# Gated attention and expert layer on one core: two full-width products written as four products of 32 weights' columns

## The reference, cut to what matters

```
x: (128, 64, 128)   ctx: (128, 64, 128)   16 heads of 8, all fp32
xn  = layernorm(x)
qh, kh, vh = heads(xn @ W_q + b_q), heads(ctx @ W_k + b_k), heads(ctx @ W_v + b_v)
ctx_out = softmax(qh kh^T / sqrt(8)) vh               # within each of the 128 sequences of 64
x   = x + tanh(g_xattn) * (ctx_out @ W_o + b_o)       # "attention's output product"
f   = layernorm(x)                                     # 8192 rows
idx, score = argmax and max of softmax((f @ w_red) @ wg_n^T)      # one of 8 experts for each row
h   = gelu(f @ W1[idx] + b1[idx])                      # 128 -> 256, "first layer"
o   = (h @ W2[idx] + b2[idx]) * score                  # 256 -> 128, "second layer"
out = x + tanh(g_ffn) * o
```

## Time and profile before

| what | us |
|---|---|
| median of 3 runs | 360.19 |
| lowest, highest | 358.85, 363.16 |
| the profiled execution, whole | 359.64 |
| its span, first to last instruction | 357.2 |
| mean granted TensorE clock over the span | 0.974 |

### The profile page before, as it was taken

One profiled execution on the slowest core, in us unless ns is written; L12 is line 12 of the kernel. 1 busy time (PEld: TensorE's weight loads), 2 busy tenths in 40 slices (PEclk: granted clock), 3 DMA queues, 4 the chain that ended last, 5 costly groups with the idle time before them and its releaser, 6 DMA issues.

```text
span 357.2 us, 15462 instructions
## 1 busy us (share of the span) xinstructions
PE 311.2 (87%) x5630; PEld 234.2 (66%) x5630; DVE 285.5 (80%) x1024; ACT 240.9 (67%) x604; POOL 260.7 (73%) x417
## 2 busy tenths in 40 slices
PE   3978899998999899999999977677798999999950
PEld 1625766775775676776776655566687889998840
DVE  7787989889899989989999899978577666666620
ACT  3666699898889879999988973746333555555520
POOL 6585755386386888898899878786777777777771
PEclk9989999999999999999999999989989999999995
DMA  5344535334413423323212121251124443433110
GB/s 118 97 142 115 136 119 143 101 99 105 122 62 94 152 76 110 102 72 117 76 59 67 54 86 44 71 158 50 57 77 136 141 129 104 114 106 98 58 41 0
DMA packets 47157, 34.01 MB, mean 95 GB/s; under 512 B 9800, under 2 KB 42955, under 8 KB 47083
## 3 DMA queue, kind: packets, MB, share of 16 engines
q1 hardware_dynamic: 42440, 23.90, 24.1%
q0 software_dynamic: 4352, 9.00, 7.5%
q10 hardware_dynamic: 292, 0.13, 0.1%
HBM read 17.13 MB, written 10.04 MB: 76 GB/s over the span
## 4 chain that ended last, share of the span: by engine, by line
PE 57%; POOL 11%; DVE 10%; issue 9%; ACT 7%; SPq 2%; DMA 1%; POOLq 0%; DVEq 0%; ACTq 0%
PE m L1354 9%; PE sc L1326 8%; POOL records L437 6%; PE sc L1188 6%; PE pv L1263 6%; PE pv L1275 4%; PE m L1418 4%; PE m L1411 4%; PE sc L1198 3%; PE sc L1181 3%; DVE mx L1046 2%; PE m L1287 2%; POOL out L512 2%; PE m L1351 2%; ACT PT L636 2%
## 5 line engine op out<-in xcount | busy, mean ns | idle before, releaser
L1046 DVE TENSOR_REDUCE mx<-sc 128x8 f32<-128x512 f32 x128 | 82.1, 683 | 14.1 <-PE sc L1198 13.8
L512 POOL DMA_INDIRECT out<-fo,rr x71 | 69.8, 983 | 22.7 <-issue 20.6
L437 POOL DMA_INDIRECT records<-XR,pos x64 | 63.3, 990 | 17.0 <-issue 15.8
L636 ACT ACTIVATE PT<-sc 128x512 f32<-128x512 f32 x64 | 38.1, 595 | 21.2 <-issue 15.5
L1354 PE MATMUL m<-w,fgT 128*128 x280 | 49.7, 301 | 0.1
L1326 PE MATMUL sc<-fxT,w1s 128*128 128x128 f32 x276 | 44.2, 283 | 5.0 <-ACT fxT L619 2.6
L1025 DVE SCALAR_TENSOR_TENSOR fo<-m,rr 128x128 f32<-128x128 f32 x70 | 24.4, 349 | 27.1 <-PE m L1354 26.9
L1263 PE MATMUL pv<-PT,V 128*32 128x64 f32 x2048 | 42.6, 223 | 2.4 <-DVE NV L1066 1.4
L1326 PEld LDWEIGHTS sc<-fxT,w1s 128*128 128x128 f32 x276 | 37.1, 195 | 7.5 <-issue 4.4
L1188 PE MATMUL sc<-Qd,kT 32*128 32x128 f32 x1024 | 40.1, 273 | 0.0
L619 ACT ACTIVATE fxT<-sc 128x128 f32<-128x128 f32 x69 | 19.1, 277 | 31.1 <-PE sc L1314 30.5
(11 more groups left out here) (225 smaller groups left out, 729.4 us busy)
## 6 DMA issues: line engine op xcount, KB each, us to landing
rr<-records SPq DMA_DIRECT2D x71, 72.0 KB, 2.1
XC<-in_x SPq DMA_DIRECT2D x16, 256.0 KB, 4.3
C<-in_ctx SPq DMA_DIRECT2D x16, 256.0 KB, 3.7
Qd<-Qf SPq DMA_DIRECT2D x64, 64.0 KB, 1.9
Kd<-kb SPq DMA_DIRECT2D x64, 32.0 KB
w<-in_L_ffn_W SPq DMA_DIRECT2D x16, 128.0 KB, 2.8
out<-fo,rr POOLq DMA_INDIRECT x71, 2.3
w1l<-in_L_ffn_W SPq DMA_DIRECT2D x8, 128.0 KB, 3.7
```

What stands on the lines that cost most here:

```text
L437: nc.gpsimd.indirect_dma_start(out=records, out_offset=bass.IndirectOffsetOnAxis(ap=pos[:, u:u + 1], axis=0), in_=XR[:, u, :], in_offset=N ...
L512: nc.gpsimd.indirect_dma_start(out=out_rows, out_offset=bass.IndirectOffsetOnAxis(ap=rr[q][:, R_ID:R_ID + 1].bitcast(U32), axis=0), in_=fo ...
L636: nc.scalar.activation(pt[:, 0:2], sc[:, 0:2, 256:512], ACT.Exp)
L1046: nc.vector.tensor_reduce(mx[c % 2][:, t:t + 2, HI * u:HI * u + HI], sc[:, t:t + 2, 0:256].rearrange("p t (i k) -> p t i k", i=HI), AX_X, ...
```

## The change

Each of the two products is written as RT = 4 products of 32 weights' columns, which write 32 partitions each (`q` or `32 * t`), with the same moving data. The arithmetic and the buffers are the same, and so are all waits: the first of the four has the wait that the one product had, and the last counts the semaphore up. The program of the other engines is unchanged. The first-layer weights `w1s` are still copied whole.

```diff
@@ values(k) @@
                 if 0 <= no < NU:
                     pe.wait_ge(ot_ok, no + 1)
-                    last = nc.tensor.matmul(attn_out(k), OT[no % 2][:, :], wox[:, :], start=True, stop=True,
-                                            skip_group_check=True)
+                    for t in range(RT):
+                        q = slice(32 * t, 32 * t + 32)
+                        last = nc.tensor.matmul(attn_out(k)[q, :], OT[no % 2][:, q], wox[:, :], start=True, stop=True,
+                                                skip_group_check=True)
@@ f_hidden(k) @@
                 for m in range(HH):
-                    i = nc.tensor.matmul(hidden(k)[:, P * m:P * m + P],
-                                         w1s[p][:, P * m:P * m + P],
-                                         fxT[p][:, :], start=True, stop=True, skip_group_check=True)
+                    for t in range(RT):
+                        q = slice(32 * t, 32 * t + 32)
+                        i = nc.tensor.matmul(hidden(k)[q, P * m:P * m + P], w1s[p][:, P * m + 32 * t:P * m + 32 * t + 32],
+                                             fxT[p][:, :], start=True, stop=True, skip_group_check=True)
```

## The result

The changed kernel takes **367.74 us** (median of 4 runs, 367.01 to 368.46), the kernel before in the same session 359.81 us (median of 4, 358.85 to 363.16). The ratio is **1.020, 95% interval 1.015 to 1.025**: 2.0% slower, where 360.6 was forecast and 364.4 was the upper end of the range. The profiled execution after took 368.46 us with a span of 366.7. Some executions of every kernel fall into a slower state; the medians here are over all runs and the ratios over those outside it, so that a ratio can differ a little from the quotient of two medians.

The account below looks back on a forecast made before the run. PE, with ACT at the seams and POOL second, was taken to bound attention, and POOL's scatters the expert part; attention -2.3 and expert part +2.7 (5.1 - 2.4) gave +0.4 on the median 360.19, 360.6 us, range 357.4 to 364.4.

Parts of the forecast that it names:

- The views it read: Whole kernel: seams 0.05 us after ACT, 0.32 spare at j = 3; POOL's round 13.07; POOL limits expert part at 1.28.
- its second bound: Expert part: two-tile loop through `fo`, `fx`, `w1s`, first and second layer, 2.60 + 0.1 = 2.7 us, 1.35 per tile.
- Streaming and entries on PE: Both products: splitting streams no faster; only width changes cost, 0.20 into full width, 0.13 into 32 columns, 0.11 for bf16.
- The lower bound of 0.09 for the emptying: First layer: least cost of entering 32-column tiles, for the emptying alone; 0.13 us was taken, upper bound 0.20.
- Attention, -2.3 us: Output product: 1.9 us saved up to POOL's last wait, then 0.15 and perhaps 0.3 more; bounds 1.0 and 2.8.
- The failed step: First layer: 24 more instructions ahead of the register load cost 0.1 us on the two-tile loop; 1.38 us per tile.
- The backlog: Expert part's end: of POOL's 3.68 us lag behind results, 2.4 cover part of the tiles' 5.1 us loss.
- The second: Expert loop: entry, later register load and DVE's stall add up, 1.48 us per tile, 365.5 us; chance 0.15.
- The first rival: Expert part: PE's tile stays below POOL's at 1.27 us, attention's gain stands alone, 357.9 us; chance 0.14.
- the fourth: Both products: nothing changes the entries, j = 2 and 3 win nothing, tiles lose, 362.9 us or more; chance 0.06.
- the third: Attention: keeps its whole gain, 10.6 us, giving 352.7 us; middle case 4.1 us and 358.8; chance 0.07.
- What would show it: Profile after: no step before output product, j = 3 seams 0.05, round 13.07, turns 1.36 or more apart, scatters lag about 1.

Follow-up runs that it names:

- the kernel with one load: Changed kernel with one register load for all tiles, so every tile uses the first tile's expert: 363.09 us, ratio 1.004 to the kernel before.
- the four kernels with the tiles: Output product in 32-column tiles, POOL's additions unchanged: changed kernel 367.74 us, register load ahead of first layer 363.14, one register load 363.09, first layer whole 359.76.
- the load ahead: Changed kernel with PE's register load of the expert's number issued ahead of the first layer: 363.14 us, ratio 1.0025 to the kernel before.
- wide addition only: Kernel before, POOL's four additions to `XR` per chunk's norm made one of 512 columns: ratio 1.014 on a slow chip; elsewhere 363.64 us, 1.008.
- two tiles of 64 columns, load ahead: Kernel before with first layer in two 64-column tiles and register load ahead of it, output product whole: 363.68 us, ratio 1.009; slow chip 1.002.
- attention's tiles only: Kernel before with only the output product in 32-column tiles, first layer whole: 359.76 us, ratio 0.995; slow chip 1.007.
- the wide addition from chunk 4: Kernel before with POOL's four norm additions made one of 512 columns from chunk 4 on only: 362.17 us, ratio 0.9965.

## Why the prediction was wrong, and where it was right

- **Where the miss lies.** In the profiled pair the expert part was put at +2.7 us and came to +8.8, attention at -2.3 and came to +0.7. Of the 6.1 in the expert part 4.3 are tiles 18 to 67, 1.2 the first 18, 0.6 the last three.
- **The views it read** held: ACT's 0.05 us at the seams, POOL's round of 13.07, the spare 0.32 of the j = 3 slots. One reading did not. "In the expert part POOL is the limit outright" is true of the last scatter. But POOL lagged by 3.2 us, some 2.5 tiles, where the buffers allow 16, and PE's step of 1.30 hung on the wait for `w1s`, the register load behind it and the bias product 0.26 us behind that. The prediction had that loop as its second bound.
- **Streaming and entries on PE** held. The output product lost its entry (0.43 to 0.23), the logits follow at their own width (0.22 in the chain of the kernel with one load, 0.34 before), and the tile's own step came out at 1.348 and 1.363 us once the load was not in its way, where 1.12 + 0.24 = 1.36 had been worked out. The switch into narrower tiles shows as 0.09 more behind the turn (0.20 for 0.11), less than the 0.13 taken for it. The lower bound of 0.09 for the emptying is worked out from no row, and no run shows it by itself.
- **Attention, -2.3 us**: measured alone 0.5% or 1.8 us, interval 0.3 to 3.4. The mechanism is borne out in both parts, the gain at the j = 3 seams and the hold of POOL's round. The size is not: PE's 0.3 to 0.45 us more behind slot 27 did not come, and from slot 3 to the first expert result the four kernels with the tiles take 203.4, 203.1, 202.9 and 202.7 us for 203.4 before, so that the traces show 0 to 0.7 us. In the profiled pair the start was 0.97 later, slots 3 to 58 1.69 shorter, slots 58 to 63 1.20 longer with the half-clock stretch, the way to the first result 0.2 longer: 0.67 in all. Start and stretch are chance of one execution as far as known, and the prediction had put no term for them.
- **The failed step** is in the part on the first layer: "PE's sequencer issues 24 instructions more per tile ahead of the register load; ... and I take 0.1. It lies on the two-tile loop", whence 1.38 us a tile. The sequencer was seen, but priced by how fast it issues. What happens is that the register load waits until the first layer begins on the array, and its 0.30 us and the 0.26 to the bias product then come behind that start. It is not beside the array's entries but on top of them: 1.348 + 0.142 = 1.490 us. In place of 50 x 0.10 = 5.0 us, tiles 18 to 67 lost 9.33; with the load ahead they lose 2.40, so that 6.93 go with the load's late start. The first 18 tiles, put at 0.1, lost 1.27; but with the first layer alone changed, and the load as late, they lost 0.36, and other kernels spread from 30.5 to 32.8 us there for 32.04 before, so that this part stays open.
- **The backlog**: 2.4 us were to be covered, 2.32 were, in the changed kernel.
- **The sum without the failed step** would have given the right time, but in part by luck: the kernel with the load ahead is the changed kernel less the late load, and it is at +0.9 us (-0.8 to +2.6) beside the kernel before, where +0.4 was forecast. Its expert part is 2.70 us longer, just as forecast, but from other terms: 2.40 from the loop, 0.92 less in the first 18 tiles, 0.39 more in the last three, and POOL's lag grew by 0.82 where 2.4 were to be covered.
- **The rivals.** The second, "the entry, the later load of the expert's number and DVE's stall add up in place of overlapping", is what came: 1.48 us a tile against 1.49, and 365.5 against 367.7, at a chance of 0.15. The reason given against it, that the sequencer's 0.1 and PE's entries overlap, is the one that fell. Its number was right in part by luck: it took 0.13 for the entry and 0.05 for the rest, and 0.05 (1.348 for 1.299) and 0.142 were measured. No row shows DVE's stall on the path, but it is not ruled out: `fx` takes 0.42 us on the mean before, 0.39 in after and 0.34 with the load ahead, so that the stalls went together with the late load. The first rival fell (the step stayed above 1.28), the fourth too, since the output product lost its entry; the third fell with POOL's round.
- **What would show it**: the seams, the round, the output product and the turn's step of at least 1.36 came as listed (1.46). The scatters at the end lag by 1.36 us rather than 3.68, near the "about 1 us"; most of those before the last three by 0.8.

## What to carry to other kernels

When a group of instructions is split in four, look at what the sequencer has to do behind it, and at a register load above all: with 32 instructions ahead of it, it started only when the array got to that group, with 16 it did not. Issued ahead of the group it cost no time here. Splitting a product into column tiles streamed no faster; here it paid only where the neighbours have the same width, and where they don't it left the step 0.05 us longer, even with the load out of the way. A stage that another engine's round holds gives its gain only when that round is shortened too, and moving that engine's work can cost elsewhere, here in the first slots: read both before adding gains up. And compare profiled executions stretch by stretch: what lies ahead of the change, the clock at the start above all, differed by more than the change was worth.

## What the hardware showed that was not expected

- PE's register load of 0.30 us starts 0.023 us behind the first weight load of a 32-instruction group, in nearly every tile of the loop; with 8 instructions it mostly starts 0.075 us behind the wait ahead of the group. With 16, on a slow chip, it is like with 8 (57 of 71 tiles within 0.08 us of the wait). The late start cost 0.142 us per tile on the mean. Where between 16 and 32 it sets in was not tried.
- PE stops in the middle of a row of matmuls that wait for nothing. In the kernel with one load:

```profile
76.37 0.54 PE L1263 MATMUL pv<-PT,V 128*32 128x64 f32 x24 [0.76 <-issue]
80.55 0.25 PE L1263 MATMUL pv<-PT,V 128*32 128x64 f32 x2 [0.62 <-issue]
```

  In twelve profiled executions off the slow chips there are 13 such stops of 0.3 to 0.8 us, all between 75 and 95 us, and each ends 1.24 to 1.52 us behind the landing of a 16 KB packet on the instruction queue, of which before has 46 and after 56. That they are late fetches of instructions is argued from this, not shown. An execution has none to three of them. They are in the table above, because they hide part of what attention's tiles save up to slot 27: the four kernels with these tiles and POOL's old round stand still for 0.5 to 1.7 us.
- The quarter more time on the slow chips may have to do with this; it was not tested. PE was idle there for 32.8 us, 39 times, ahead of weight loads of the values' product alone, for nothing that the profile shows (wide addition only; the granted clock of that execution was 0.873):

```profile
PEld pv L1262 <- issue: 32.8, 39, 3.9
```

- The first scores start at 32.5 to 34.3 us in most profiled executions, but at 34.9 in one (two tiles of 64 columns, load ahead) and at 36.0 to 36.1 in three, and these four then have 11.00 instead of 9.93 us in slots 0 to 3, in all 3.5 to 4.7 us against before. It goes with the clock, whatever the kernel: between 19 and 38 us the granted clock is 0.73 in the one and 0.55 in the three, and 0.82 to 0.91 in the others. The three are at 1.2 GHz for 17.1 us on end, from 19.7 to 20.2 us on, the one for 10.2, the others for 3.4 or twice that. The windows view of before and of attention's tiles only (stretch and its length, PE busy, granted clock, DMA, GB/s):

```profile
19.00:38.00 19.00, 14.86 (x215) 0.91 0.50 143
19.00:38.00 19.00, 16.99 (x139) 0.55 0.48 135
```

  Why the clock stayed down in these four was not found; it is as large as any gain here. Two of them, attention's tiles only (364.24 us) and the wide addition from chunk 4 (365.24), are the longest executions of their kernels.
